# A token, attention and feed-forward kernel with a rewritten beginning: loads spread out, patch sums last in their group, an empty tile left out

## What is computed

```
h = layernorm(patches16(x)) * ln1_g + ln1_b      # 64 x 196 x 768
h = layernorm(h @ W + b) * ln2_g + ln2_b         # 64 x 196 x 256
h = concat([h, txt], axis=1)                     # 64 x 273 x 256
y = layernorm(h); Q, K, V = y @ W.T + b, each as (n, head, token, d), 16 heads of 16
s = einsum('nqhd,nkhd->nhqk', Q, K) / 4          # so h runs over tokens, q and k over heads
a = einsum('nhql,nlhd->nqhd', softmax(s), V)     # (n, head, token, d), read as (n, token, 256)
h = h + a @ Wo.T + bo
n = layernorm(h); p = n shifted by one token
r = sigmoid((mu_r*n + (1-mu_r)*p) @ W_r.T)
k = relu((mu_k*n + (1-mu_k)*p) @ W_k.T) ** 2
out = h + r * (k @ W_v.T)
```

## Time and profile before

| | |
|---|---|
| median of 3 runs | 1607.35 us (1607.32 to 1609.72) |
| profiled execution | 1607.39 us, its span 1605.3 us |
| mean granted TensorE clock | 0.951 |
| PE, DVE, ACT, POOL busy | 87%, 77%, 70%, 57% |
| DMA | 243.43 MB, mean 152 GB/s |

### The profile page before, as it was taken

How to read it: one execution, slowest core, us unless ns; L and a number is a source line. 1 busy time by engine, 2 the same in 40 slices (tenths; PEclk the granted TensorE clock), 3 DMA queues, 4 the chain that set the end, 5 groups by cost and what they waited for, 6 DMA issues and landing times. The chain is left out here.

```text
span 1605.3 us, 51258 instructions
## 1 busy us (share of the span) xinstructions
PE 1399.5 (87%) x17678; PEld 1312.6 (82%) x17678; DVE 1237.2 (77%) x3109; ACT 1120.5 (70%) x2410; POOL 920.5 (57%) x1593
## 2 busy tenths in 40 slices
PE   1568979898999899999899989998999999998976
PEld 1567878788889888988888888898888888888875
DVE  4468777778888788878787888798788888886652
ACT  2357576767876778778767776777677768766754
POOL 2133146557566574765566656655657656666676
PEclk8678989999999999999999999999999999999987
DMA  8149898688898889968986889699897879779830
GB/s 244 40 117 172 167 180 140 141 148 153 173 174 162 134 161 174 167 139 165 176 156 136 178 155 167 132 175 156 170 177 140 172 157 170 151 145 144 163 63 30
DMA packets 687537, 243.43 MB, mean 152 GB/s; under 512 B 589682, under 2 KB 658354, under 8 KB 687154
## 3 DMA queue, kind: packets, MB, share of 16 engines
q1 hardware_dynamic: 687281, 240.16, 78.3%
HBM read 137.18 MB, written 107.94 MB: 153 GB/s over the span
## 5 line engine op out<-in xcount | busy, mean ns | idle before, releaser
L1765 PE MATMUL bank<-wqkv,xnT 128*128 128x384 f32 x1656 | 337.0, 348 | 5.2 <-DVE probs L1492 1.8
L1765 PEld LDWEIGHTS bank<-wqkv,xnT 128*128 128x128 f32 x1656 | 285.1, 191 | 14.2 <-issue 5.5
L1869 PE MATMUL bank<-wtok,xT 128*126 128x258 f32 (+1 forms) x1800 | 255.2, 298 | 0.0
L1869 PEld LDWEIGHTS bank<-wtok,xT 128*126 128x126 f32 (+1 forms) x1800 | 236.9, 200 | 0.0
L1405 POOL TENSOR_TENSOR mixp<-mixf,mixp 128x384 fp32r<-128x384 f32 x184 | 185.2, 1014 | 83.1 <-ACT mixp L1741 82.6
L1662 ACT ACTIVATE arena<-qk,ymask 128x384 f32<-128x384 f32 x368 | 203.2, 609 | 41.5 <-DMA qk<-qkv_dram 31.5
L1683 ACT ACTIVATE xcols<-xim 84x640 f32<-84x640 f32 (+1 forms) x192 | 121.4, 692 | 80.6 <-DVE xs L1511 44.8
L1584 DVE TENSOR_TENSOR qkvt<-bank,bqkv 128x384 f32<-128x384 f32 x276 | 148.7, 546 | 29.8 <-PE bank L1765 20.2
L1420 POOL TENSOR_TENSOR h<-h,r 128x256 f32<-128x256 f32 x138 | 102.0, 743 | 94.7 <-DVE r L1621 93.7
L1349 POOL TENSOR_TENSOR rs<-ve,small 126x1 f32<-126x1 f32 (+1 forms) x192 | 135.1, 704 | 15.0
L1347 POOL TENSOR_TENSOR ve<-mv,small 126x1 f32<-126x1 f32 (+1 forms) x192 | 37.4, 195 | 174.7 <-DVE mv L1545 87.0
(11 more groups left out here) (119 smaller groups left out, 3229.6 us busy)
## 6 DMA issues: line engine op xcount, KB each, us to landing
qkv_dram<-qkvt SPq DMA_DIRECT2D x138, 384.0 KB, 3.4
xim<-in_x SPq DMA_DIRECT2D x128, 294.0 KB
qk<-qkv_dram SPq DMA_DIRECT2D x46, 768.0 KB, 8.3
arena<-qkv_dram SPq DMA_DIRECT2D x368, 48.0 KB
hc<-h_dram SPq DMA_DIRECT2D x45, 384.0 KB, 4.8
out<-h SPq DMA_DIRECT2D x45, 384.0 KB, 3.5
o_dram<-probs SPq DMA_DIRECT2D x108, 96.0 KB, 2.3
on<-o_dram SPq DMA_DIRECT2D x73, 128.0 KB
```

The lines of the kernel that those rows point to most:

```text
L1765: ins = mm(psum, left(a, k), right(b, k), start=t == 0, stop=t == len(terms) - 1)
L1869: ins = mm(place("tok", 0, t)[0:pr, 0:E + 2], xT[:, a, ch, :, :].rearrange("p i w -> p (i w)")[:, r0:r0 + pr], wtok[:, b, ch, :], start=n ...
```

## The change

The step tables are rewritten. All operations keep their order, on every engine, but for the four text copies: they stood at steps 3, 4, 5 and 7, ahead of and just behind the load of image 0, and now stand behind the load of image 2, behind the `hin` of chunk 5, of chunk 16 and of chunk 28. The other step numbers shift by up to four.

The rest of the diff, cut to its core:

```
+USED = [-(-rows // TT) for rows in OUT_ROWS]
...
+    def skip(self, eng, k, steps):
+
+        self.wait(eng, k, steps)
+        eng.sem_inc(self.sem, self.unit)
...
-        WEIGHTS_AT = []
-        for t in (1, 1, 2, 2, 2, 3, 3):
-            WEIGHTS_AT.append(min(AT["tok"][0][t] + 1, AT["xt"][0][0]))
+        weights_at = min(AT["h"][0][2] + 1, AT["xt"][0][0])
...
-        TOK_RAWS, RAWS = 4 + 2 + 1, 2 + 4 + 7
-        DVE_SUM = KCH + 1
+        TOK_RAWS, RAWS = 4, 2 + 4 + 7
+        DVE_SUM = KCH
...
-                    sp.dma_start(lnt[:, 6 + 3 * c:9 + 3 * c], ln1_b[384 * c:384 * c + 384].rearrange("(p c) -> p c", c=CH)).then_inc(raw_tok, 16)
-                sp.dma_start(c0b[:, :], tok_b.rearrange("(a e) -> a e", a=1).broadcast_to((128, E))).then_inc(raw_tok, 16)
+                    sp.dma_start(lnt[:, 6 + 3 * c:9 + 3 * c], ln1_b[384 * c:384 * c + 384].rearrange("(p c) -> p c", c=CH)).then_inc(raw_bias, 16)
...
+            def load_rest(m):
+
+                if m == 0:
+                    load_vector(c0b[:, :], tok_b, raw_c0)
+                    load_vector(g2b[:, :], ln2_g, raw_ln)
+                    load_vector(b2b[:, :], ln2_b, raw_ln)
+                    for n in range(3):
+                        load_square(n)
+                if m == 1:
+                    for x, v in enumerate((bq, bk, bv)):
+                        load_vector(bnat[:, x, :], v, raw_in)
+                    for n in range(3, 5):
+                        load_square(n)
+                    for n in range(5, 7):
+                        load_square(n)
...
+                    load_vector(bob[:, :], bo, raw_in)
...
-                    if m == 0:
-                        load_rest()
+                    load_rest(m)
```

On DVE:

```
-            dve.wait_ge(prep_dve, c)
-            prep(V.tensor_reduce(wsum, scaled.rearrange("p c e -> p e c"), AX.X, ALU.add))
+            dve.wait_ge(raw_bias, 2 * 16)
...
             dve.wait_ge(prep_pe, 2)
+            dve.wait_ge(raw_c0, 16)
```

On PE:

```
-            pe.wait_ge(prep_dve, DVE_SUM)
-            mm(banks[SPARE[0]][:, 0:E], ones, wsum, start=True, stop=True).then_inc(prep_pe, 1)
-            pe.wait_ge(raw_tok, TOK_RAWS * 16)
-            pe.wait_ge(prep_dve, DVE_SUM + KCH)
             for ch in range(KCH):
-                ins = mm(banks[SPARE[1]][:, 0:E], c0rep[:, ch, :], raw[:, ch, :], start=ch == 0, stop=ch == KCH - 1)
+                pe.wait_ge(prep_dve, ch + 1)
+                ins = mm(banks[SPARE[0]][:, 0:E], ones, scaled[:, ch, :], start=ch == 0, stop=ch == KCH - 1)
             ins.then_inc(prep_pe, 1)
+
+            def token_bias():
+                pe.wait_ge(prep_dve, DVE_SUM + KCH)
+                for ch in range(KCH):
+                    ins = mm(banks[SPARE[1]][:, 0:E], c0rep[:, ch, :], raw[:, ch, :], start=ch == 0, stop=ch == KCH - 1)
+                ins.then_inc(prep_pe, 1)
...
                         x_tr.done(ins)
+                        if job == 1 and m == 0:
+                            token_bias()
...
-                    x_stats.wait(pe, m, 1)
+                    x_lo.wait(pe, m, 3 * X_PARTS[m])
                     turn("tok", 0, t)
-                    for m in patch_images(t):
...
-                    x_lo.wait(pe, m, 3 * X_PARTS[m])
...
                     for n, (a, b, ch) in enumerate(terms):
...
+                    x_stats.wait(pe, m, 1)
+                    for m in patch_images(t):
...
                     tok_pe.done(ins)
```

In eight places (`qkv`, `wo`, `r` and `val` on PE; `qb`, `h2` and `rv` on DVE; `rt` on ACT) stands what follows, with the signal of that place, so that the third tile of chunk 45 is not computed:

```
+                        if i >= USED[k]:
+                            qkv_pe.skip(pe, k, job)
+                            continue
```

More of the change, by code:

```diff
@@ L1138, in fusion_kernel @@
         block = ctx.enter_context(nc.Block())
-        WEIGHTS_AT = []
-        for t in (1, 1, 2, 2, 2, 3, 3):
-            WEIGHTS_AT.append(min(AT["tok"][0][t] + 1, AT["xt"][0][0]))
+        weights_at = min(AT["h"][0][2] + 1, AT["xt"][0][0])
         def weights_due(s):
-            return [n for n, v in enumerate(WEIGHTS_AT) if v == s]
+            return range(len(WEIGHTS)) if s == weights_at else []
         raw = arena[:, 0:PDIM // 128 * E].rearrange("p (c e) -> p c e", c=KCH)
@@ L1186, in load_rest, with load_square @@
-                    for n, w in enumerate(WEIGHTS):
-                        sp.dma_start(rawsq[n], w.rearrange("(a p) e -> p a e", p=128)).then_inc(raw_in, 16)
-                    for s, v in ((0, mu_k), (1, mu_r)):
-                        sp.dma_start(mus[:, s, :], v.rearrange("(k p) -> p k", p=128)).then_inc(raw_in, 16)
+                    sp.dma_start(dst, v.rearrange("(a e) -> a e", a=1).broadcast_to((128, E))).then_inc(signal, 16)
+            def load_square(n):
+                sp.dma_start(rawsq[n], WEIGHTS[n].rearrange("(a p) e -> p a e", p=128)).then_inc(raw_in, 16)
@@ new lines, in load_rest @@
+            def load_rest(m):
[12 more added lines that the diff above has]
+                        load_square(n)
+                    with nc.allow_non_contiguous_dma(reason="small vectors, once"):
+                        for side, v in ((0, mu_k), (1, mu_r)):
+                            sp.dma_start(mus[:, side, :], v.rearrange("(k p) -> p k", p=128)).then_inc(raw_in, 16)
+                    load_vector(bob[:, :], bo, raw_in)
@@ L1578, in _ @@
                         i, half = job // 2, job % 2
+                        if i >= USED[k]:
+                            qkv_sb.skip(dve, k, job)
+                            continue
                         qkv_pe.wait(dve, k, job + 1)
@@ L1592, in _ @@
                     for k in due(s, "h2", i):
+                        if i >= USED[k]:
+                            h2_sb.skip(dve, k, i)
+                            continue
                         c = k % SLOTS
@@ L1618, in _ @@
                     for k in due(s, "rv", i):
+                        if i >= USED[k]:
+                            rv_sb.skip(dve, k, i)
+                            continue
                         val_pe.wait(dve, k, i + 1)
@@ L1752, in _ @@
                     for k in due(s, "rt", i):
+                        if i >= USED[k]:
+                            r_tanh.skip(act, k, i)
+                            continue
                         r_pe.wait(act, k, i + 1)
@@ L1855, in _ @@
                     m = patch_images(t)[-1]
-                    x_stats.wait(pe, m, 1)
+                    x_lo.wait(pe, m, 3 * X_PARTS[m])
                     turn("tok", 0, t)
-                    for m in patch_images(t):
-                        i0 = TROWS * t - GRID * m + PAD
-                        mm(place("tok", 0, t)[0:pr, E + 2:E + 2 + GRID],
-                           imask[:, :, :].rearrange("p i w -> p (i w)")[:, GRID * i0:GRID * i0 + pr],
-                           xs[:, m % 2, :], start=m == patch_images(t)[0], stop=m == patch_images(t)[-1])
-                    x_lo.wait(pe, m, 3 * X_PARTS[m])
                     if t == 0:
@@ L1868, in _ @@
                     for n, (a, b, ch) in enumerate(terms):
-                        ins = mm(place("tok", 0, t)[0:pr, 0:E + 2], xT[:, a, ch, :, :].rearrange("p i w -> p (i w)")[:, r0:r0 + pr],
-                                 wtok[:, b, ch, :], start=n == 0, stop=n == len(terms) - 1)
+                        mm(place("tok", 0, t)[0:pr, 0:E + 2], xT[:, a, ch, :, :].rearrange("p i w -> p (i w)")[:, r0:r0 + pr],
+                           wtok[:, b, ch, :], start=n == 0, stop=n == len(terms) - 1)
+                    x_stats.wait(pe, m, 1)
+                    for m in patch_images(t):
+                        i0 = TROWS * t - GRID * m + PAD
+                        ins = mm(place("tok", 0, t)[0:pr, E + 2:E + 2 + GRID],
+                                 imask[:, :, :].rearrange("p i w -> p (i w)")[:, GRID * i0:GRID * i0 + pr],
+                                 xs[:, m % 2, :], start=m == patch_images(t)[0], stop=m == patch_images(t)[-1])
                     tok_pe.done(ins)
@@ L1897, in _ @@
                     for k in due(s, "wo", i):
+                        if i >= USED[k]:
+                            wo_pe.skip(pe, k, i)
+                            continue
                         on_lo.wait(pe, k, 2)
@@ L1917, in _ @@
                     for k in due(s, "r", i):
+                        if i >= USED[k]:
+                            r_pe.skip(pe, k, i)
+                            continue
                         mix_lo.wait(pe, k, 4)
@@ L1922, in _ @@
                     for k in due(s, "val", i):
+                        if i >= USED[k]:
+                            val_pe.skip(pe, k, i)
+                            continue
                         ka_lo.wait(pe, k, 2)
```

10 lines of the change are left out of this document (4 added, 6 removed), and 752 rows, old and new, of tables (add, av, carry, d).

## The result

The changed kernel took 1587.63 us (median of four runs, 1583.16 to 1592.09), the kernel before beside it 1607.34 (four runs, 1601.36 to 1609.72): a ratio of 0.9883 [0.9843, 0.9923], 1.2% faster. The forecast was 1576.5 in a range of 1561 to 1592. Direction and range hold; of the 30.9 us of gain that were forecast 19.7 came. The profiled execution took 1583.2, its span is 1581.3.

The account below looks back on a forecast made before the run. PE's work was taken to pace the long middle, something else the first 100 us. Terms -31.0 (start), -2.3, -2.7 and +5.1 (text copies) sum to -30.9, from 1607.4 to 1576.5 us; range 1561 to 1592.

Parts of the forecast that it names:

- (a): Start: DVE's preparation no longer waits for ln1_b and tok_b, beginning at 5.5 us instead of 8.40 (bounds 5.0 and 8.4).
- (b): Start: DVE's scaling takes 4.2 us, to 9.8; PE adds six parts at 0.7 each instead of the reduce; bias columns end 11.1.
- (f): Start: image 1's load lands at 16.5, so its copies begin at 22.3, not 39.50: 17.2 us gained.
- (g): Start: tile 1's 18 matmuls run under DVE's sums of image 1; tile 2 takes 2.39 us, to 40.2.
- (h): Start: all seven square weights in one block; image 3's copies end at 53.3 instead of 84.3, gain 31.0 us.
- The transition: Tile group at 114.71 behind the start: PE runs its matmuls during the 2.33 us wait for sums, -2.3 us.
- The middle's sums: Middle: PE's 5.3 us of waits for DVE's patch sums vanish; half reaches the end, -2.7 us (bounds 0 and -5.3).
- The text copies: Middle: three text copies behind row loads delay what is queued behind, 1.7 us each, +5.1 us (bounds 0 and 23).
- Rival C: Text copies hold the queue at their 7.8 us each, nothing absorbed: 1595 us; chance 0.06.
- The last tile: Last chunk: the empty tile's some 4.4 us saves nothing, as the end hangs on POOL: 0 (bounds 0 and -4.4).
- A: Rival: the weight block eats its part, only image loads and early start steps won, 17.2 us: 1590 us; chance 0.15.
- B: Rival: start and middle at higher clock, all middle waits and last tile won, texts free: 1559 us; chance 0.15.

Follow-up runs that it names:

- after_third: The changed kernel run again without edit, in the third group: median 1588.70 us, ratio 0.9891 to the kernel before.
- copies_doubled: The changed kernel plus three more text copies, into a DRAM tensor nobody reads, behind the `hin` of chunks 10, 22 and 34: 1600.81 us, ratio 0.9965.
- tile_kept: The changed kernel with the empty third tile of chunk 45 computed as before: 1590.06 us, ratio 0.9895.
- Sums first: The changed kernel with the sum matmuls put back ahead of the tile's 18 matmuls: 1593.43 us, ratio 0.9927.
- texts_gaps: The changed kernel with its text copies behind loads 2 and 3, chunk 0's rows and load 5, none in the middle: 1583.14 us, ratio 0.9856.
- texts_early: The changed kernel with all four text copies back at the start, behind loads 2 to 5: 1585.94 us, ratio 0.9868.
- weights_spread: The changed kernel with the seven square weights at their old places, behind tiles 1, 2 and 3: 1599.38 us, ratio 0.9944.
- texts_only: The kernel before with only the four text copies moved, to the changed kernel's places: 1605.63 us, ratio 0.9968.
- gaps_and_memset: The changed kernel with no text copy in the middle and POOL's clearing held back until after DVE's preparation: 1582.23 us, ratio 0.9807.
- memset_late: The changed kernel with POOL's clearing MEMSET held back behind DVE's weight preparation: 1594.58 us, ratio 0.9880.

## Why the prediction was right or wrong, step by step

**The start, right in mechanism, 3.0 us too much.** In the first profile all the miss is in (a) and (b).
- (a) DVE begins at 6.90, not 5.5; the other profiles have 6.0 to 7.0. The forecast's own numbers, issued until 2.6 and 3.3 us to land, add up to 5.9.
- (b) failed on two counts. The 4.2 us of the earlier trace rows are a sum over six pieces, and one of these took 2.7 us; I took the sum for a cost that moves along with its start. It is not DVE's own time: it ends when POOL's MEMSET ends, and that stands at 7.7 to 11 in both kernels. To start DVE earlier only put more of it under the MEMSET (3.5 us); where it began at 6.0, the bias columns were held in place of the scaling, and the sum was read at 12.0. And PE was dearer: it ran its parts in 2.90 us before DVE's long piece and 2.93 behind it, the last of it ending at 14.20, where 0.7 a part behind DVE was forecast. Together DVE reads the sum at 14.23 instead of 11.1.
- (c) From that read to the last split 5.0 was right (14.23 to 19.24). (d) PE's bias term took 2.79, not 4.2, and stayed hidden; image 0 was copied at 9.89, forecast 9 to 10. (e) DVE reached image 0 at 19.97, the 3.2 us later that (a) and (b) make.
- (f) Image 1's copies at 25.52, bound by DVE's sums as forecast, 14.0 us gained instead of 17.2. The ten small DMAs and the squares had no price.
- (g) and (h): tile 1 under DVE's sums; tile 2 in 2.39 us, the full clock, right behind them; weights in one block at 47 to 54, image 3's copies at 54.09. Up to the end of image 3's copies this part gave 14.3 us where 13.8 were forecast, up to `bn` 14.0.

That holds for the first profile. In after_third and copies_doubled (a) and (b) cost only 1.4 and 1.3 us (the sum is read at 12.49 and 12.44), and `bn` is where it was, at 62.62 and 62.74, with tiles 2 and 3 at the half clock. So the 28.0 us repeat, but what is won before 20 us is not carried on one for one, as the prediction assumed. In tile_kept, which had both the earlier sum and tile 2 at 2.38 us, `bn` is at 60.63.

On tile 2 the Trainium skill's rule that transposes don't count as busy for the clock (*TensorE: Matmul & The Clock Gate*, Part 4) would have allowed the half clock, 1.8 us more. The traces show both: the full 2.4 GHz level in four profiles, the half in five, each time behind the same 18 matmuls, 4 sums and 5 transposes of the same code. So the rule alone does not decide this place, and the forecast's 2.39 was right in four of nine.

**The transition (-2.3), wrong.** The wait at 114.71 is gone, as forecast, and the shift did not grow (26.9 at chunk 2). The shift changes by -1.5 to +0.9 us there in nine profiles. The step took an idle gap on PE for time of the path. POOL's `hb<-hc,bob` of chunk 2 waits for DVE's `bn` in the changed kernel, as before, and PE's lead did not bring that forward.

**The middle's sums (-2.7, bounds 0 and -5.3), not told from nothing.** The waits vanished. Sums first cost 3.1 us in all, 1.9 of it at the start by `bn`: 1.2 is left for transition and middle together, where 5.0 was forecast. With ± 5.1 on the 3.1 the runs exclude neither; what speaks against the 5.0 is that the shift does not grow behind the start.

**The text copies (+5.1), too small.** To take them out of the middle won 5.5 us in texts_gaps and in texts_early, whose starts are 0.8 and 1.3 us later, so 6 to 7; to add three cost 10.6. Three copies' worth by the firmest pair, six copies against none, is 8 us (5.7 to 10.5). That is 2 to 4 us a copy against 1.7, and 3 at the one place where fourteen profiles can be compared. The term multiplied the landing by the share of chunks in which PE waited for returned rows. But a copy stands in one queue with q/k/v, row and image loads as well. That it delays these too is my reading; which wait grows is not shown. The 2.3 us for all three that an estimate by *DMA: Bandwidth & Descriptors* of the Trainium skill gave is further off still. Rival C, 7.8 each, falls as well: three extra copies cost 10.6, not 23, and six 16.1, not 47.

**The last tile (0), right**, and for the reason given.

**The sign named ahead.** The prediction was to be wrong if the shift at `bn` isn't found at the end too. It is 28.0 to 28.1 at chunk 0, and 24.7, 17.0 and 21.0 at chunk 45 in the three profiles of the changed kernel: the most of it is found, not all.

**Rivals.** A falls by weights_spread, and by 28.0 us at `bn` where it has 17.2. Its time, 1590, is nearer to the measured 1587.63 than the forecast's 1576.5. That the range held is in part luck: the room left for A took up a loss that has other causes. B falls: tiles 0 and 1 took 4.10 and 3.71 us, mostly at the half clock, and nothing that the runs show came of the middle or the last tile. D (12 us a copy) falls by copies_doubled, and E, the small vectors, by texts_only, which moves the texts alone and has image 0 at 11.28.

**The account.** -28.0 at the start, -1.2 for transition and middle, +6 to +10.6 for the copies: -19 to -23, where -15.4 to -18.8 were measured by means, and -19.7 by the first medians. Against the forecast of -30.9 the start gave 3.0 less, transition and middle 3.8 less, and the copies cost 1 to 5.5 more.

**Open.** Up to 8 us of this account remain. In nearly all full variants 2 to 5 us of the shift go between chunks 2 and 3 (147 to 216 us of the kernel before), also where no text copy stands there (27.7 to 23.6 in texts_gaps, 26.8 to 22.6 in texts_early), and hardly in gaps_and_memset (29.8 to 28.5) or in texts_only (12.6 to 11.4), which has a copy there. The second profile of the kernel before loses 2.1 against the first there, so part of it may be the first profile's own. Some of it comes back by chunk 8. Neither the copies, nor the place of the sums, nor the tile explains it, and with code-identical profiles 6.0 us apart I can't separate it from scatter. Nor is it settled why texts_early loses 7 us on the way with no copy in the middle.

## What to carry to other kernels

Before a group's summed duration is moved, look at its shortest and longest piece: one that is ten times the others is waiting for somebody, and goes with that one, not with its own engine. An idle gap removed on the busiest engine counts only where the next engine in the chain was waiting for it. A large transfer is cheapest where the queue's next entry is one that nobody waits for; one copy just ahead of the rows that DVE needed brought them 2 us later. And a gain at the start may be lost at once to a lower clock of the next groups: look at more than one profile before it is added up.

## What the hardware showed that I had not expected

- **POOL's plain MEMSET holds a DVE instruction up.** A DVE scaling of 128x256 float32, 0.35 us by itself, took 3.5 us beside a 3.33 us MEMSET of 128x3840 by POOL, and 2.7 us in the kernel before beside one of 3.29; never over 0.40 with the MEMSET moved. Only one instruction is held, and until about the end of the MEMSET; it may be a smaller one (128x128, 3.45 us in place of 0.27). Not every form is held: in memset_late the same MEMSET, at 17.36 to 20.66, ran beside DVE's `xT<-bank,xT` TENSOR_TENSORs, which took 1.10 us for two, as elsewhere. The Trainium skill (*GPSIMD Engine Reference*, 1. Specifications) says that POOL shares its SBUF interfaces with VectorE, with contention for DVE instructions in a two-port mode or with two SBUF inputs; that agrees in kind. It gives no size, and which of its two conditions holds here no run shows.
- **Two identical programs wander by 5 us on the way and come back.** The two profiles of the kernel before are 6.0 us apart at chunk 24 and 1.2 at the end of the span. A loss seen in one profile between two markers proves little below that.
- **The same code gets either clock level.** Tile 2, behind the same instructions, took 2.38 to 2.39 us in four profiles and 3.94 to 4.09 in five; the granted clock of that stretch was 1.00 in the first profile and 0.55 in after_third.
